# Last tile of a DLRM tower: two corner transfers move from ScalarE's queue to GpSimd's, and the last first layer is issued around tile 14's second layer

## The reference

```python
e = jnp.stack([tbl_0[ids[:, 0]], ..., tbl_49[ids[:, 49]]], axis=1)   # (2048, 50, 16)
gram = jnp.einsum('bid,bjd->bij', e, e)
z = gram[:, _I_IDX, _J_IDX]                                          # the 1225 pairs i < j
h = jnp.concatenate([z, dense_ctx], axis=1)                          # 1241 features
h = jnp.maximum(h @ W_top1 + b_top1, 0.0)                            # 1241 -> 512
h = jnp.maximum(h @ W_top2 + b_top2, 0.0)                            # 512 -> 256
y = h @ W_top3                                                       # 256 -> 1
```

## Time and profile before

| | |
|---|---|
| median of 3 runs | 453.33 us (450.83 to 456.07) |
| profiled execution, its own time | 453.39 us |
| its span, first to last instruction | 451.3 us |
| outside the span | 2.1 us |
| TensorE busy | 342.9 us (76%) |
| VectorE busy | 295.8 us (66%) |
| ScalarE busy | 198.8 us (44%) |
| GpSimd busy | 322.7 us (71%) |
| mean granted TensorE clock | 0.890 |

### The profile page before, as it was taken

One profiled execution on the slowest core, in us unless ns is written; L12 is line 12 of the kernel. 1 busy time (PEld: TensorE's weight loads), 2 busy tenths in 40 slices (PEclk: granted clock), 3 DMA queues, 4 the chain that ended last, 5 costly groups with the idle time before them and its releaser, 6 DMA issues.

```text
span 451.3 us, 13158 instructions
## 1 busy us (share of the span) xinstructions
PE 342.9 (76%) x5633; PEld 247.4 (55%) x5633; DVE 295.8 (66%) x606; ACT 198.8 (44%) x288; POOL 322.7 (71%) x318
## 2 busy tenths in 40 slices
PE   0568167566488979979989699798895948989886
PEld 0567067565366657666666476656653525454543
DVE  2599899999357579758576687566715437165551
ACT  2335712246235774455457653445487324140511
POOL 5788777777777777787777777778777777776020
PEclk9978659978679997989999969699998895988999
DMA  6994503423321344243213433111121222212020
GB/s 161 407 367 142 173 7 101 118 77 86 82 44 39 104 115 94 63 136 88 47 32 103 115 95 65 36 43 36 40 53 24 66 50 50 48 15 61 5 61 1
DMA packets 24638, 38.92 MB, mean 86 GB/s; under 512 B 8532, under 2 KB 15876, under 8 KB 24452
## 3 DMA queue, kind: packets, MB, share of 16 engines
q1 hardware_dynamic: 14166, 35.04, 24.0%
q0 software_dynamic: 9920, 2.55, 6.6%
q10 hardware_dynamic: 494, 0.49, 0.3%
HBM read 26.98 MB, written 0.14 MB: 60 GB/s over the span
## 4 chain that ended last, share of the span: by engine, by line
PE 34%; DVE 18%; ACT 13%; SPq 11%; issue 10%; DMA 8%; POOL 5%; another core or an unknown queue 0%; DVEq 0%; ACTq 0%; POOLq 0%
PE hid_ps L881 12%; SPq L383 11%; DVE onehot L490 9%; PE look_ps L803 8%; ACT gram L1010 6%; POOL emb L448 5%; DMA ids_bc<-ids_dram 5%; PE mid_ps L938 5%; PE gram_ps L820 3%; ACT z_both L1077 2%; DVE turned L604 2%; PE gram_ps L841 2%; ACT looked L1047 2%; DMA z_both<-gram 2%; DVE w_sb L672 1%
## 5 line engine op out<-in xcount | busy, mean ns | idle before, releaser
L448 POOL DMA_INDIRECT emb<-tbl,gidx x304 | 318.9, 1049 | 95.7 <-issue 88.4
L881 PE MATMUL hid_ps<-w_sb,z_both 127*128 127x512 f16 x462 | 112.3, 386 | 0.0
L803 PE MATMUL look_ps<-parts,onehot 125*128 125x64 f16 x1836 | 75.0, 203 | 44.5 <-DVE onehot L490 29.9
L490 DVE TENSOR_SCALAR onehot<-ids_bc,rows 125x2048 f16<-125x2048 f16 (+1 forms) x144 | 92.2, 690 | 19.2 <-PE look_ps L803 14.7
L803 PEld LDWEIGHTS look_ps<-parts,onehot 125*128 125x128 f16 x1836 | 69.5, 105 | 56.2 <-issue 20.8
L1010 ACT ACTIVATE gram<-gram_ps 50x784 f32<-50x784 f32 x96 | 78.2, 815 | 29.6 <-PE gram_ps L820 26.7
L803 PE MATMUL look_ps<-parts_med,onehot 125*128 125x128 f16 x800 | 57.1, 233 | 14.4 <-DVE onehot L490 13.8
L881 PEld LDWEIGHTS hid_ps<-w_sb,z_both 127*128 127x128 f16 x462 | 41.5, 99 | 46.1 <-issue 3.3
L803 PEld LDWEIGHTS look_ps<-parts_med,onehot 125*128 125x128 f16 x800 | 53.1, 105 | 20.6 <-DVE parts_med L663 13.9
L490 DVE TENSOR_SCALAR onehot<-ids_bc,rows_med 125x1024 f16<-125x1024 f16 x100 | 45.8, 495 | 28.2 <-PE look_ps L803 24.4
L1047 ACT ACTIVATE looked<-look_ps 128x1024 f16<-128x1024 f32 (+1 forms) x28 | 26.7, 954 | 67.0 <-PE look_ps L803 66.6
(11 more groups left out here) (74 smaller groups left out, 221.7 us busy)
## 6 DMA issues: line engine op xcount, KB each, us to landing
ids_bc<-ids_dram SPq DMA_DIRECT2D x28, 512.0 KB
emb<-tbl,gidx POOLq DMA_INDIRECT x304
z_both<-gram SPq DMA_DIRECT2D x31, 121.0 KB
z_both<-w SPq DMA_DIRECT2D x1, 2816.0 KB
z_both<-gram SPq DMA_DIRECT2D x31, 90.8 KB
z_both<-gram SPq DMA_DIRECT2D x152, 6.2 KB
z_both<-gram SPq DMA_DIRECT2D x31, 60.5 KB
gram<-small SPq DMA_DIRECT2D x2, 512.0 KB, 5.1
```

The lines of the kernel that those rows point to most:

```text
L448: pool.indirect_dma_start(emb[:, T % TPC, f, :], None, big[f], bass.IndirectOffsetOnAxis(ap=gidx[:, T, f:f + 1], axis=0)).then_inc(landed, 16)
L490: nc.vector.tensor_scalar(onehot[0:TP, s % RING, 0:cnt, :], ids_bc[0:TP, o % IDS_BUFS, 0:cnt, :], row, None, ALU.is_equal).then_inc(onehot ...
L803: last = nc.tensor.matmul(bank[:, half, at:at + width], onehot[0:TP, at_ring, i, t * TILE:(t + 1) * TILE], moving.rearrange("p i s d -> p ...
L881: return nc.tensor.matmul(hid_ps[:, :], z_parts[0:KP, T % 2, x, k, :], w1_sb[0:KP, k, w, :], start=(i == 0), stop=(i == L1_MM - 1))
```

## The change

Two edits, both in the last tile's path.

1. The split of the packing transfers. `BIG_PIECES` becomes the four large pieces, `CORNERS` the five small ones. SyncE still issues six transfers of side 0, the same ones in the same order. ScalarE issues the four large ones of side 1, no corner. GpSimd issues eight corners: three of side 0 and then all five of side 1. ScalarE's wait in `split_last(0)` counts accordingly.
2. TensorE's order. The first layer of tile 15 is taken out of `last_mlp` into `last_layer(i)`; its first part is issued ahead of tile 14's second layer, its second part behind it.

```diff
-BIG_PIECES, CORNERS = PIECES[:6], PIECES[6:]
+BIG_PIECES, CORNERS = PIECES[:4], PIECES[4:]
+SP_CORNERS = 2
+POOL_PIECES = [(0, p) for p in CORNERS[SP_CORNERS:]] + [(1, p) for p in CORNERS]
...
-            pack(NTILES - 1, (0,), BIG_PIECES)
+            pack(NTILES - 1, (0,), BIG_PIECES + CORNERS[:SP_CORNERS])
...
-            for a in range(TWO):
-                for piece in CORNERS:
-                    out, src = piece_of(piece, LAST, a)
-                    pool.dma_start(out, src).then_inc(corners_in, 16)
+            for a, piece in POOL_PIECES:
+                out, src = piece_of(piece, LAST, a)
+                pool.dma_start(out, src).then_inc(corners_in, 16)
...
+            def last_layer(i):
+
+                T = LAST
+                ks = LAST_KS[i]
+                pe.wait_ge(z_hi, T + 1 + i)
+                for k in ks:
+                    for w in range(2):
+                        nc.tensor.matmul(hid_last, z_parts[0:KP, T % 2, 0, k, :], w1_sb[0:KP, k, w, :],
+                                         start=(k == 0 and w == 0), stop=False)
+                pe.wait_ge(z_split, T + 1 + i)
+                for k in ks:
+                    last = nc.tensor.matmul(hid_last, z_parts[0:KP, T % 2, 1, k, :], w1_sb[0:KP, k, 0, :],
+                                            start=False, stop=(k == ST - 1))
+                if i == len(LAST_KS) - 1:
+                    last.then_inc(mlp_done, 1)
...
             mlp(LAST - 1, TURN_STEP)
+            last_layer(0)
             mlp(LAST - 1, L2_STEP)
+            last_layer(1)
             last_mlp()
...
-                    act.wait_ge(packed[T % 2], PIECE_INC * (T // 2 + 1) - 16 * TWO * len(CORNERS))
-                    act.wait_ge(corners_in, 16 * TWO * len(CORNERS))
+                    act.wait_ge(packed[T % 2], PIECE_INC * (T // 2 + 1) - 16 * len(POOL_PIECES))
+                    act.wait_ge(corners_in, 16 * len(POOL_PIECES))
```

## The result

The changed kernel takes 457.14 us (median of 6 runs, 456.58 to 458.88), the kernel before 453.56 us in the same comparison (6 runs, 450.83 to 456.07). The ratio is 1.008, with a 95% interval of 1.0041 to 1.012: 3.6 us slower, within one per cent, clear of noise. The profiled execution took 457.22 us with a span of 455.2 us and a mean granted clock of 0.891, against 0.890 before.

A forecast was written before the change was run, and what follows sets the result against it. TensorE, gapless from 435.27 to 444.40 us, was taken as the bound. Starting its 9.12 us at 436.15, the earlier landing included, ends 0.9 us later: 453.39 + 0.9 = 454.3, median forecast 454.2, range 451.5 to 457.5.

The forecast's parts named there:

- the clock rival: TensorE's longer hole before tile 15 makes its clock fall: 1.8 to 3.4 us more, 456.0 to 457.6; chance 0.22.
- the unedited rest moves by more than all this: Sign that the prediction is wrong: time of the unedited rest of the program moves by more than the forecast effects.
- S: Issue of SyncE's first packing transfer for tile 15, from which the prediction counted its signs in the profile.
- The second layer loses its cover: TensorE idles until tile 15's split, tile 14's ready second layer standing behind; its work ends 0.9 us later.
- ScalarE starts at about 435.3 instead of 435.49: 0.2 us earlier: Start of tile 15's split on ScalarE, GpSimd's eighth corner landing last at 435.25; bounds 434.5 and 435.65.
- GpSimd held up by VectorE: GpSimd's eighth corner issue delayed beside VectorE's activation: shift +1.2 to +1.4 us, 454.8; chance 0.06.
- The early landing: Tile 15's packing transfers all there by 434.2 or 433.6: 453.2 or 452.6 us; chance 0.12.
- The waits with room: Tile 15's low part and second half, and tile 14's score, are ready before their use and cost nothing.

The follow-up runs named there:

- e2: Changed kernel with TensorE's old order restored, so only the new transfer split differs from the kernel before: 453.72 us, ratio 1.0009 against before.
- e7: Kernel before with all ten corners issued by GpSimd, four large transfers each on SyncE and ScalarE, old TensorE order: 450.05 us, one execution.
- e8: Changed kernel with all ten corners issued by GpSimd, four large transfers each on SyncE and ScalarE, new TensorE order: 458.14 us, one execution.
- e3: Unedited copy of the kernel before: 453.01 us, ratio 0.999 against before.
- e1: Changed kernel with the old transfer split (6, 6, 6), so only TensorE's new order differs from the kernel before: 455.47 us, ratio 1.0029 against before.
- e4: Unedited copy of the changed kernel: 455.36 us, ratio 1.0058 against the kernel before.

## Why the prediction was right, and where it was not

The time lies in the range and on the forecast side (slower, within 1%), but the change cost 3.6 us where 0.9 were forecast. The forecast's own bounds, 453.5 to 454.7 us, were missed; 457.1 is in the range only because it reaches to the upper end of the clock rival. By one of its own signs, that the unedited rest moves by more than all this, the first profile counts against it too: 2.46 us lie ahead of S. Point by point:

**The second layer loses its cover: right.** This step held. TensorE idles behind the transposes, is released by the split, and then works through the same five pieces; e2 against after shows the order alone to decide, with equal transfers. The shift behind S was 1.40 us at full clock against +0.9.

**"ScalarE starts at about 435.3 instead of 435.49: 0.2 us earlier": this step failed.** With the new transfers the split came 0.2 to 0.6 us later than before (six profiles, S + 7.11 to 7.52 against S + 6.88). The working took the median landing of 2.5 us for GpSimd's eighth corner "since the new two are issued when the large transfers are mostly through", and took SyncE's six as unchanged. The changed kernel's row reads

```profile
L473 POOL DMA_DIRECT2D z_both<-gram x8: 497/513/557, 431.6 to 435.2; - x8
DMA to landing us min/median/max: 2.3/2.5/2.9
```

and its chain names a transfer of SyncE's queue as the last, landing 3.31 us after its issue at 435.00, while in the kernel before it had to be there by S + 6.88, 2.96 us after its issue at the same place. That it is SyncE's is inferred: SyncE's and ScalarE's transfers raise the same semaphore (`packed`; GpSimd's alone raise one of their own), and the profile names the last one issued. The packets agree, since ScalarE's end first. GpSimd's eighth was no better: it took 2.8 to 3.2 us to land in the six profiles (2.9 here, to S + 7.06), where 2.5 was taken; rows 3 had 2.9 as their upper end. SyncE's last took 3.2 to 3.6 us, where 1.99, measured on ScalarE's lone last corner, was taken. So the mis-sized terms are these two landings, which put the split at S + 7.1 to 7.5 instead of 6.7. That three queues which end together delay each other's landing is a reading of this. For it speaks that GpSimd's tenth, alone at the end, landed after 1.9 us in e7 and 2.3 in e8; no run varied this alone. The late split makes up the 0.5 us between 0.9 and 1.4.

**The clock rival: mis-sized in its chance, and hardly in its price.** It had 0.22, and four of five profiles of the new order show the fall. The price was bounded by 1.8 and 3.4 us; 1.69 was measured, just below. The argument against it ("dense matmuls follow on either side") was no argument: the fall comes in the middle of those dense matmuls. The working put the 2.5 us of idleness out of 3.15 between two rows, 1.7 us (kept) and 2.7 (fell), as if they were bounds. The other traces show that they are not. These are windows of two stretches that no edit touches, the first two of e7 (2.67 us of idleness), the last two of e3 (1.80):

```profile
285.55:288.15 2.60, 0.00 (x0) 0.00 (x0) 2.60 (x5) 2.55 (x4) 2.19 (x2) 1.00 0.10 6
288.25:291.00 2.75, 2.75 (x84) 2.54 (x85) 2.45 (x8) 1.98 (x3) 2.14 (x3) 1.00 0.11 12
235.40:237.10 1.70, 0.04 (x4) 0.04 (x8) 1.61 (x3) 1.65 (x4) 1.40 (x2) 1.00 0.10 7
238.70:241.80 3.10, 3.10 (x9) 2.20 (x9) 0.00 (x0) 0.78 (x1) 2.49 (x3) 0.50 0.78 220
```

The longer one kept the clock, the shorter one lost it. The kernel before has both stretches, at 282.2 us (2.67, fell) and at 233.3 (1.75, kept, in rows 6). Over the fourteen profiles the longer one is followed by a fall in four and not in ten. So a row says that a fall is possible, not that it comes, and a chance needs many executions of one stretch. The new hole (2.28 us behind 0.88 and the transposes, or 2.09 in e1) has it in four of five. If that were its rate, the new order with these transfers would cost 1.4 + 0.8 x 1.69 = 2.8 us. The three comparisons gave 3.6, 2.1 and 3.4 us between medians, and ratios of 1.008, 1.0058 and 1.0062, with 1.0062 (2.8 us) inside all three intervals. They would fit a lower rate too: two of three, as in the changed kernel's own profiles, gives 2.5.

**The 2.46 us ahead of S: not the change's.** S lies between 425.22 and 431.36 us over fourteen profiles; its mean is 428.5 in the seven with the old order or the cut second layer and 429.1 in the seven with the new, and the copy of before and e2 alone differ by 4.5. The first pair of profiles by itself would have put 2.5 us on an edit that, as far as the fourteen show, had none of it. What moves S from one execution to the next, beyond that the clock falls at other places in each, was not studied.

**GpSimd held up by VectorE: did not happen.** The eighth issue took as long as the others (497 to 557 ns for all) beside VectorE's activation at 435.49. **The early landing: did not happen** in any of the new splits, though the last packet ended 0.2 to 0.6 us earlier. **The waits with room had it:** tile 14's score ran at 445.05 and nothing waited for it.

## What to carry to other kernels

Before putting work ahead of a ready piece of work on the same engine, ask when its data is there, not whether it is more urgent: the order pays only if the data is there before the other work could start, and here it came 1.5 us too late (S + 8.16 against S + 6.66). Count a hole in TensorE once for its length, and once more, times a chance, for the clock of the work behind it; look for the chance in as many executions as there are, since the same stretch kept the clock in ten and lost it in four. And the last packet of a transfer is not its landing: here the split followed it by up to 1.3 us. And cut two profiles at a point which both share before any of the difference is put down to an edit.

## What the runs showed of the hardware

In e4 TensorE's clock fell behind the hole only after 1.1 us of dense work at 1.00, so that the cost of 1.69 us shows on instructions that did not cause it. Nine unused matmuls in the hole kept it, in both profiles that had them. The Trainium skill, DMA: Bandwidth & Descriptors, section Issuing engines are not separate DMA queues, says that transfers from different engines interleave on the same transfer engines and that spreading them saves only issue time. The runs agree: with ScalarE's list shortened from 5.60 to 4.08 us, the issue time was saved, and the split started at S + 7.1 to 7.6 instead of S + 6.9.
